# A float32 attention block on one core: the first group's setup reordered across five engines

## The chip, the cores and the metric

The kernel runs on one core of a Trainium2 chip. Its time is the device time of one execution, in microseconds (us). Five engines run their own instruction streams and meet only at semaphores: TensorE (PE), VectorE (DVE), ScalarE (ACT), GpSimd (POOL) and SyncE (SP), which only issues transfers. ACT issues some transfers too.

## The reference, cut to what matters

The input x has 64 batches of 128 tokens with 512 features. There are 16 query heads of 64, and one key and one value head, shared by all.

```
xn  = layernorm(x) * g_in
q   = xn @ Wq   (16 heads of 64), scaled by 64 ** -0.5
k,v = xn @ Wkv, with one null key and null value put in front (null_kv = cond_64[0], cond_64[1])
sim = q k^T + [null_attn_bias[h], attn_bias[h]]; causal and by-batch masks set entries to -max
out = softmax(sim) v;  out = out @ Wo;  y = layernorm(out) * g_out;  return x + y
```

The mask is a row per batch, attn_bias is 16 x 128 x 128 and shared by all batches.

## The kernel before, in words

Two batches make a group (32 groups), two groups a pair (16 pairs). Every matrix product is made of three with float32r operands: high part by high part, high by low, low by high. So each weight has to be split once into a high part (a rounding copy, times g_in for Wq and Wkv) and a low part (the difference). `wq_high(i)` on ACT and `wq_low(i)` on DVE split quarter i of Wq in four instructions each; a quarter serves two of the eight Q tiles of a group. `wo_high(i)` is on ACT, `wo_low(0)` and `wo_low(1)` on POOL, `wo_low(2)` and `wo_low(3)` on DVE.

Of a group PE makes: x turned (8 transposes, in the first two groups only; later groups are turned by 16 small transfers and one DVE transpose, `split_x` and `turned`), the key and value tile ("kv"), eight Q tiles, scores of two tiles at a time (`scores`), values (`values`), and the output projection of each batch (`project_out`). A "tile" is four heads of one batch: a group has eight of them, numbered t = 0 to 7 here. For each tile POOL adds the mask to the bias (`bias`), DVE adds the bias to the scores and takes the row maximum (`logits`), ACT takes exponentials (`soft`), DVE inverts the sums (`inverse`), POOL multiplies (`normalize`), and DVE transposes the weights for the product with v (`turn`).

The bias must first be prepared in place by POOL, once, in two halves (`make_bias(0)`, `make_bias(1)`): subtract the null bias of the head, add the causal mask.

There is no scheduler: each engine's order is written out by hand, and every engine runs its list strictly in order. The loop over pairs has a peeled first pair, ahead of which every engine has its own `first_group()`. PE's list there ends with the last Q tile of the second group that is made early, (1, 5), a wait for Wo's low parts, and `project_out(0)`, L559. What sets that: DVE's `heads_lo(0, g)`, which stand in DVE's list behind `turned(BY_PE)` (x of group 2, turned), which waits for the 16 transfers of `split_x(BY_PE)` on SP, which wait for ACT's `x_norm(BY_PE, 0)`. BY_PE is 2. After this point the pipeline has its steady order.

The loads ahead of the first group: SP issues x of group 0, Wkv, the four quarters of Wq, eight parts of attn_bias (four of 128 KB, the lower 64 rows in 512-byte runs, and four of 64 KB, the upper-left blocks in 256-byte runs), x of group 1, its mask, then Wo. ACT issues g_in, the null key and value, the mask of group 0, and the null bias in two transfers whose runs are 8 bytes long, each read by 64 partitions. PE multiplies an identity 30 times (WARM) while nothing is there for it.

Of the kernel before, what the change touches and what calls it, by code (L numbers as in the profile page):

```python
# [11 lines left out]
P = 128  # L12
# [8 lines left out]
WP = 4  # L21
# [37 lines left out]
WARM = 30  # L59
# [9 lines left out]
def attention_block(nc, x, attn_bias, null_kv, mask, g_in, null_bias, wq, wkv, wo, g_out, out):  # L69
# [4 lines left out]
    with ExitStack() as ctx:  # L74
# [21 lines left out]
        bias_c = sb("bias_c", [P, CB, BOT + TOP])  # L96
        nb_row = sb("nb_row", [P, CB, 2])
# [69 lines left out]
        ld_cols, ld_rows = sem("ld_cols"), sem("ld_rows")  # L167
# [13 lines left out]
        filled = sem("filled")  # L181
        waits_taken = sem("waits_taken")
        wkv_hi_made, wkv_lo_made = sem("wkv_hi_made"), sem("wkv_lo_made")
        wq_hi_made, wq_lo_made, wo_hi_made = sem("wq_hi_made"), sem("wq_lo_made"), sem("wo_hi_made")
# [26 lines left out]
        COL_LOADS, ROW_LOADS, BIAS_LOADS, V_LOADS = 4, 2, 8, 8  # L211
# [78 lines left out]
        def bank_of(slot, kind, i):  # L290
            return ps_proj[(slot + (i if kind == "x" else USE[kind, i])) % 2]

        def proj_count(f, kind, i):

            before = USES * f + XT * (min(f, BY_PE - 1) + 1 if isinstance(f, int) else BY_PE)
            return before - XT + i + 1 if kind == "x" else before + USE[kind, i] + 1

        def halves_of(f, slot, i, from_pe):

            k = slice(KX * i, KX * (i + 1))  # L300
            if from_pe:
                turned = bank_of(slot, "x", i)[:]
            else:
                turned = x_turned[:, k].rearrange("p k n -> p (k n)")
            return turned, *(xt[:, slot, k].rearrange("p k n -> p (k n)") for xt in (xt_hi, xt_lo))

        def front_parts(p, t, first, last):
            if t >= CP:
                return
            for kind, i, ahead in FRONT.get(t % CG, ()):  # L310
                if last and t // CG + ahead == 2:
                    continue
                yield 2 * p + t // CG + ahead, (t // CG + ahead) % 2, kind, i

# [3 lines left out]
        def _(sp):  # L318
# [56 lines left out]
            for i in range(WP):  # L375
                sp.dma_start(raw_piece(i, KT), wq_piece(wq.rearrange("(k p) n -> p k n", p=P), i)).then_inc(ld_wq[i], 16)
            by_head = attn_bias.rearrange("(c u e) i j -> u e i c j", u=2, e=2)
            for u in range(2):
                up = slice(HALF * u, HALF * (u + 1))
                for e in range(2):  # L380
                    sp.dma_start(bias_c[up, :, N * e:N * (e + 1)], by_head[u, e, HALF:N]).then_inc(ld_bias, 16)
                    sp.dma_start(bias_c[up, :, BOT + HALF * e:BOT + HALF * (e + 1)],
                                 by_head[u, e, 0:HALF, :, 0:HALF]).then_inc(ld_bias, 16)
            load_x(0, 1)
            load_mask(0, 1)
# [50 lines left out]
        def _(pe):  # L436
# [66 lines left out]
            def front(f, slot, kind, i):  # L503
                ps = bank_of(slot, kind, i)
                by_pe = isinstance(f, int) and f < BY_PE
                if kind == "x":
                    wait(pe, q_made, QT * f - XT + i + 1)
                    if i == 0:
                        wait(pe, xn_made, GB * (f + 1))
                    for j in range(KX * GB):  # L510
# [787 lines left out]
```

## Time and profile before

| | us |
|---|---|
| median of 3 runs | 1069.09 |
| the three runs | 1069.54, 1069.09, 1062.03 |
| the profiled execution | 1064.88 |
| its span | 1063.0 |
| mean granted TensorE clock over the span | 0.989 of full |

The profiled execution lies between the runs. Its span begins at the first instruction; 1.9 us lie around it. All times of instructions below count from the span's start. Busy time is the time an engine had an instruction in work; what stands behind an arrow in brackets is how long the engine had been idle before the instruction and what ended that.

### The profile page before, as it was taken

The numbers are of one execution on the slowest core, as the hardware profiler recorded it, in microseconds if no ns is written. First come the engines' busy times: TensorE is split into PE (matmuls) and PEld (weight loads), VectorE is DVE, ScalarE is ACT, GpSimd is POOL, SyncE is SP. The second block draws the span as 40 slices with busy tenths as digits, with TensorE's granted clock in tenths as the row PEclk, the third lists the DMA queues.
The fourth block names the chain that finished last, engine by engine and source line by source line (L and its number), as shares of the span: only waits on it lengthen the run. The fifth ranks groups of instructions, "written<-read, shape, count | busy, mean of one in ns | idle before, by whom it ended". The sixth has DMA issues, their size and how long they took to land.

```text
span 1063.0 us, 42980 instructions
## 1 busy us (share of the span) xinstructions
PE 1029.5 (97%) x14254; PEld 902.9 (85%) x14254; DVE 765.8 (72%) x3513; ACT 661.2 (62%) x2620; POOL 828.9 (78%) x1488
## 2 busy tenths in 40 slices
PE   6789999999999999999999999999999999999986
PEld 6678898888888888888888888888888889889875
DVE  4777777777777777786777787776777777777663
ACT  5655675666675665675665676565676565666552
POOL 2867887778878778878778788788788778787775
PEclk8999999999999999999999999999999999999998
DMA  7312222232222222222223122223222223121101
GB/s 213 124 34 86 77 81 89 67 94 76 63 85 82 74 87 73 68 84 85 76 82 91 50 87 84 86 70 89 62 78 85 83 73 93 54 84 59 50 25 60
DMA packets 90013, 84.01 MB, mean 79 GB/s; under 512 B 21568, under 2 KB 64064, under 8 KB 89792
## 3 DMA queue, kind: packets, MB, share of 16 engines
q1 hardware_dynamic: 88336, 81.03, 25.3%
q8 instruction: 138, 2.26, 0.9%
q14 instruction: 83, 0.68, 0.2%
q10 hardware_dynamic: 1456, 0.04, 0.1%
HBM read 40.11 MB, written 16.78 MB: 54 GB/s over the span
## 4 chain that ended last, share of the span: by engine, by line
PE 89%; issue 2%; POOL 2%; ACT 2%; DVE 1%; POOLq 0%; DVEq 0%; ACTq 0%
PE ps_proj L500 38%; PE ps_pv L488 33%; PE ps_s L452 9%; PE ps_pv L477 9%; ACT exp_bot L914 1%; POOL w_nrm L1112 1%; ACT exp_top L914 1%; POOL y_out L1156 0%; POOL y_nrm L1152 0%; DVE logit_bot L608 0%; DVE o_lo L630 0%; POOL bias_b L1103 0%; ACT xn L942 0%; POOL small L1138 0%; DVE wt L624 0%
## 5 line engine op out<-in xcount | busy, mean ns | idle before, releaser
L914 ACT ACTIVATE exp_bot<-logit_bot,neg_max 128x129 f32<-128x129 f32 x512 | 201.6, 399 | 252.0 <-DVE neg_max L608 223.0
L1103 POOL TENSOR_TENSOR bias_b<-bias_c,mask_add 128x256 f32<-128x256 f32 (+1 forms) x512 | 291.9, 599 | 45.3 <-DVE neg_max L608 45.2
L500 PE MATMUL ps_proj<-xt_hi,wq_hi 128*128 128x256 f32 x1024 | 302.5, 295 | 7.5 <-DVE q_sb L690 6.0
L500 PE MATMUL ps_proj<-xt_lo,wq_hi 128*128 128x256 f32 x1024 | 288.6, 282 | 0.9 <-issue 0.9
L500 PE MATMUL ps_proj<-xt_hi,wq_lo 128*128 128x256 f32 x1024 | 288.6, 282 | 0.0
L608 DVE CUSTOM_DVE_ANT_0 logit_bot<-ps_s,bias_b 128x128 f32<-128x128 f32 x512 | 128.3, 288 | 180.1 <-PE ps_s L452 162.4
L500 PEld LDWEIGHTS ps_proj<-xt_hi,wq_hi 128*128 128x128 f32 x1024 | 193.3, 189 | 24.9 <-issue 13.0
L1112 POOL TENSOR_TENSOR w_nrm<-exp_bot,w_inv 128x256 f32<-128x256 f32 x256 | 156.9, 613 | 65.2 <-DVE w_inv L617 65.2
L488 PE MATMUL ps_pv<-wo_hi,o_hi 128*128 128x512 f32 x488 | 199.0, 408 | 1.2 <-DVE o_lo L630 1.2
L488 PE MATMUL ps_pv<-wo_lo,o_hi 128*128 128x512 f32 x488 | 193.5, 397 | 0.0
L500 PEld LDWEIGHTS ps_proj<-xt_hi,wq_lo 128*128 128x128 f32 x1024 | 193.4, 189 | 0.0
L488 PE MATMUL ps_pv<-wo_hi,o_lo 128*128 128x512 f32 x488 | 193.4, 396 | 0.0
L500 PEld LDWEIGHTS ps_proj<-xt_lo,wq_hi 128*128 128x128 f32 x1024 | 193.3, 189 | 0.0
L914 ACT ACTIVATE exp_top<-logit_top,neg_max 128x65 f32<-128x65 f32 x512 | 172.6, 342 | 0.0
L630 DVE SCALAR_TENSOR_TENSOR o_lo<-ps_pv,small,o_hi 128x256 fp32r<-128x256 f32 x252 | 104.5, 477 | 43.3 <-ACT o_hi L923 43.3
L624 DVE STREAM_TRANSPOSE wt<-w_nrm 128x384 f32<-128x384 f32 x256 | 131.8, 553 | 2.0 <-POOL w_nrm L1112 2.0
L452 PEld LDWEIGHTS ps_s<-keys,q_sb 64*64 64x64 f32 x4096 | 98.2, 134 | 37.8 <-issue 29.3
L690 DVE COPY q_sb<-ps_proj 128x256 f32<-128x256 f32 x252 | 105.8, 420 | 33.8 <-PE ps_proj L500 32.4
L923 ACT ACTIVATE o_hi<-ps_pv,small 128x256 fp32r<-128x256 f32 x252 | 98.3, 473 | 37.9 <-PE ps_pv L477 37.9
L452 PE MATMUL ps_s<-keys,q_sb 64*64 64x128 f32 (+1 forms) x4096 | 115.5, 251 | 5.7 <-DVE q_sb L690 2.0
L1112 POOL TENSOR_TENSOR w_nrm<-exp_top,w_inv 128x128 f32<-128x128 f32 x256 | 116.2, 454 | 0.0
L488 PEld LDWEIGHTS ps_pv<-wo_hi,o_hi 128*128 128x128 f32 x488 | 91.9, 188 | 26.8 <-issue 1.4
(94 smaller groups left out, 1778.6 us busy)
## 6 DMA issues: line engine op xcount, KB each, us to landing
x_in<-in_x_dram SPq DMA_DIRECT2D x32, 512.0 KB, 4.1
x_res<-in_x_dram SPq DMA_DIRECT2D x64, 256.0 KB, 2.9
out_dram<-y_out SPq DMA_DIRECT2D x64, 256.0 KB, 2.1
x_split<-xn SPq DMA_DIRECT2D x480, 32.0 KB, 1.9
v_rep<-v_raw SPq DMA_DIRECT2D x256, 32.0 KB, 1.9
w_raw<-in_L_cond_Wq_dram SPq DMA_DIRECT2D x4, 512.0 KB, 11.7
w_raw<-in_L_cond_Wo_dram SPq DMA_DIRECT2D x4, 512.0 KB, 5.2
mask_u<-in_mask_BxS_bk_dram SPq DMA_DIRECT2D x31, 32.0 KB, 3.7
```

The lines of the kernel that those rows point to most:

```text
L452: mm = pe.matmul(scored[HALF * u:HALF * (u + 1)], q_sb[rows, slot, t % CB + s, u, from_:from_ + HALF], keys[rows, slot, b, 0:N if late els ...
L477: mm = pe.matmul(of_tile(ps_pv[g])[DH * e:DH * (e + 1), :, late], v32[rows, slot, b, j], wt[rows, b, block], start=(r == 0), stop=(r == le ...
L488: mm = pe.matmul(out_bank(batch)[:], o[:, u, c], w[:, 2 * c + u], start=(u == 0 and j == 0), stop=(u == 1 and j == len(todo) - 1))
L500: mm = pe.matmul(ps[:, 0:TOK], w[:, k, cols], xt[:, slot, k], start=(j == 0), stop=(j == len(todo) - 1))
L608: ins = nc.vector.tensor_tensor_reduce(out_[:, e, 0:keys_], ps_s[e][:, from_:from_ + keys_], bias[:, e], -1.0, 0.0, ALU.add, ALU.min, neg_ ...
L624: nc.vector.transpose(wt[:, par, :, c], w_nrm[:, s]).then_inc(wt_made, 1)
L630: nc.vector.scalar_tensor_tensor(out=place_of(lo, g), in0=of_tile(ps_pv[g]), scalar=nv_col[:, 0:1], in1=place_of(hi, g).bitcast(F32), op0= ...
L690: nc.vector.tensor_copy(q_sb[:, slot, i // 2, i % 2], bank_of(slot, kind, i)[:, 0:TOK]).then_inc(q_made, 1)
L914: ins = nc.scalar.activation(out_[:, s, j], in_[:, s, j], ACT.Exp, bias=neg_max[:, s, k:k + 1], scale=-1.0, accum_out=w_sum[:, s, k:k + 1])
L923: nc.scalar.activation(place_of(hi, g), of_tile(ps_pv[g]), ACT.Identity, bias=nv_col[:, 0:1]).then_inc(o_hi_made, 1)
L1103: ins = nc.gpsimd.tensor_tensor(out_, bias, key_mask, ALU.add)
L1112: ins = nc.gpsimd.tensor_tensor(out_, w_exp[:, s, :, 0:keys_], w_inv[:, s, 2 * i:2 * i + 2].unsqueeze(2).to_broadcast([P, 2, keys_]), ALU. ...
```

## The change

1. **Null bias.** Instead of two transfers in 8-byte runs, one transfer brings all 16 values to each of the 128 partitions (`nb_all`, 64-byte runs); DVE puts them into `nb_row` with two copies behind `mask_of(0, 0)`, and POOL waits for these (`nb_made`).
2. **Table first.** ACT makes a small copy right behind the issue of g_in, so that its table load comes there and not at the first use.
3. **Loads.** The four 128 KB parts of attn_bias are issued by ACT, behind that copy and ahead of the null bias, null key and value and mask. SP issues Wq quarters 0 and 1, the four 64 KB parts of the bias, Wq 2, x of group 1, Wq 3, its mask.
4. **GpSimd splits part of Wq.** POOL makes the high part of quarter 1 (four instructions, ahead of `make_bias(0)`). DVE takes `wq_low(1)` ahead of the first Q copy.
5. **PE.** 50 identity products in place of 30, ten more behind the transposes; x is turned batch by batch, as soon as one batch is normalized, into two banks of their own (`ps_pv[1]`, `ps_pv[2]`); the first group's kv tile takes its eight products of the high part before it waits for the low part of x; group 1 is turned ahead of Q tile 6, not behind `scores(0, 2)`.
6. **Order of ACT, DVE and POOL in `first_group()`.** ACT: `x_norm(1, 1)` ahead of `soft(0)`, the four `wo_high` later, `x_norm(BY_PE, 0)` behind `soft(5)` (it was ahead of `soft(2)`), with `soft(6)`, `wo_high(3)`, `soft(7)` behind it. DVE: the statistics of group 1 ahead of the second Q copy, `logits(0, 0)` and `logits(1, 1)` ahead of `wq_low(3)`, `x_low_of(1)` ahead of the statistics of group 2, `wo_low(2)` and `wo_low(3)` later. POOL: `x_rstd_of(1)` between `bias(0)` and `bias(1)`.

```diff
-WARM = 30
+WARM = 50
+WARM_X = 10
...
+        def x_bank(i):
+            return ps_pv[1 + i]
...
+            load_wq(0)
+            load_wq(1)
             for u in range(2):
                 for e in range(2):
+                    load_bias_early(sp, u, e)
+            load_wq(2)
             load_x(0, 1)
+            load_wq(3)
             load_mask(0, 1)
...
+            def turn_x(f):
+                for b in range(GB):
+                    wait(pe, xn_made, GB * f + b + 1)
+                    for k in range(KT):
+                        j = GB * (k % KX) + b
+                        bank = x_bank(k // KX)[:, N * j:N * (j + 1)]
+                        mm = pe.transpose(bank, xn[:, b, P * k:P * (k + 1)], ident[:])
+                        if b == GB - 1 and k % KX == KX - 1:
+                            mm.then_inc(x_by_pe, 1)
...
             def first_group():
                 for _ in range(WARM):
                     pe.transpose(ps_s[0][:, 0:P], ident[:], ident[:])
-                for i in range(XT):
-                    front(0, 0, "x", i)
-                front(0, 0, "kv", 0)
+                turn_x(0)
+                for _ in range(WARM_X):
+                    pe.transpose(ps_s[0][:, 0:P], ident[:], ident[:])
+                key_values_of_first()
                 for i in range(4):
                     front(0, 0, "q", i)
                 scores(0, 0)
-                for i in range(4, QT):
-                    front(0, 0, "q", i)
+                front(0, 0, "q", 4)
+                front(0, 0, "q", 5)
+                turn_x(1)
+                front(0, 0, "q", 6)
+                front(0, 0, "q", 7)
                 scores(0, 2)
-                for i in range(XT):
-                    front(1, 1, "x", i)
                 front(1, 1, "kv", 0)
...
+            dve.wait_ge(ld_cols, 16 * COL_LOADS)
             nc.vector.tensor_scalar(k_shift[:], nk_col[:], -SCALE, None, ALU.mult).then_inc(shifts_made, 1)
             nc.vector.tensor_scalar(v_shift[:], nv_col[:], -1.0, None, ALU.mult).then_inc(shifts_made, 1)
             mask_of(0, 0)
+            dve.wait_ge(ld_rows, 16)
+            for u in range(2):
+                up = slice(HALF * u, HALF * (u + 1))
+                nc.vector.tensor_copy(nb_row[up], nb_all[up].rearrange("p (c u e) -> p u c e", u=2, e=2)[:, u]).then_inc(nb_made, 1)
...
                 x_low_of(0, True)
                 wq_low(0)
+                wq_low(1)
                 q_copies(0, 0)
-                wq_low(1)
+                x_stats_of(0, 1)
+                x_mean_var_of(1)
                 q_copies(0, 1)
                 wq_low(2)
                 q_copies(0, 2, 3)
+                logits(0, 0)
+                logits(1, 1)
                 wq_low(3)
-                logits(0, 0)
-                x_stats_of(0, 1)
-                x_mean_var_of(1)
-                logits(1, 1)
                 inverse(0, 0)
+                x_low_of(1, True)
                 x_stats_of(1, 0)
                 x_mean_var_of(2)
...
+            act.wait_ge(filled, 1)
+            nc.scalar.copy(y_shift[:], eps_col[:]).then_inc(table_loaded, 1)
+            for u in range(2):
+                for e in range(2):
+                    load_bias_late(act, u, e)
+            act.dma_start(nb_all[:], null_bias.partition_broadcast(P)).then_inc(ld_rows, 16)
...
-                for i in range(1, WP):
-                    wq_high(i)
-                wo_high(0)
-                q_copies(4)
-                soft(0)
-                q_copies(5, 6)
-                x_norm(1, 1)
-                q_copies(7)
-                soft(1)
-                wo_high(1)
-                x_high_of(1, True)
-                x_norm(BY_PE, 0)
-                soft(2)
+                wq_high(2)
+                wq_high(3)
+                x_norm(1, 1)
+                soft(0)
+                q_copies(4)
+                soft(1)
+                q_copies(5)
+                x_high_of(1, True)
+                q_copies(6, 7)
+                wo_high(0)
+                soft(2)
                 front(1, 1, "kv", 0)
                 soft(3)
+                wo_high(1)
+                soft(4)
                 wo_high(2)
-                soft(4)
+                soft(5)
+                x_norm(BY_PE, 0)
+                soft(6)
                 wo_high(3)
...
+                pool.wait_ge(ld_gin, 16)
+                pool.wait_ge(ld_wq[1], 16)
+                for k in range(KT):
+                    nc.gpsimd.tensor_scalar(wq_piece(wq_hi, 1)[:, k], raw_piece(1, KT)[:, k], gin_col[:, k:k + 1], None,
+                                            ALU.mult).then_inc(wq_hi_by_pool, 1)
+                pool.wait_ge(nb_made, 2)
                 pool.wait_ge(ld_bias, 16 * BIAS_LOADS)
                 make_bias(0)
                 bias(0)
+                x_rstd_of(1)
                 bias(1)
                 make_bias(1)
-                x_rstd_of(1)
```

## Rows read from the trace of the kernel before

**Rows 1.** Busy time by engine, 62 to 1020 us: PE, PEld, DVE, ACT, POOL, clock, DMA

```profile
62.00:1020.00 958.00, 955.28 (x13346) 838.51 (x13346) 705.36 (x3268) 604.77 (x2427) 766.13 (x1376) 1.00 0.25 76
```

**Rows 2.** Timeline of PE to 63 us: start, duration, instructions, idle before them

```profile
1.53 5.83 PE L535 MATMUL ps_s<-ident 128*128 128x128 f32 x30 [1.53 <-POOL ident L1163]
...
11.88 1.97 PE L512 MATMUL ps_proj<-ident,xn 128*128 128x128 f32 x8 [4.51 <-ACT xn L942]
...
15.34 0.55 PE L500 MATMUL ps_proj<-xt_hi,wkv_hi 128*128 128x256 f32 x1 [1.49 <-DVE xt_lo L670]
...
59.20 0.39 PE L500 MATMUL ps_proj<-xt_hi,wq_hi 128*128 128x256 f32 x1 [1.81 <-DVE q_sb L690]
...
62.07 0.47 PE L488 MATMUL ps_pv<-wo_hi,o_hi 128*128 128x512 f32 x1 [1.18 <-DVE o_lo L630]
```

**Rows 3.** Timeline of DVE, 21 to 61 us

```profile
21.57 1.67 DVE L712 SCALAR_TENSOR_TENSOR wq_lo<-w_raw,small,wq_hi 128x256 fp32r<-128x256 f32 x4 [0.58 <-ACT wq_hi L992]
...
23.49 3.61 DVE L712 SCALAR_TENSOR_TENSOR wq_lo<-w_raw,small,wq_hi 128x256 fp32r<-128x256 f32 x4
...
30.95 0.28 DVE L608 CUSTOM_DVE_ANT_0 logit_bot<-ps_s,bias_b 128x128 f32<-128x128 f32 x1
...
34.35 1.25 DVE L651 BATCH_NORM_STATS2 x_stats<-x_in 128x6 f32<-128x512 f32 x2
35.52 0.42 DVE L658 BATCH_NORM_AGGREGATE x_mv<-x_stats 128x2 f32<-128x6 f32 x2
...
40.75 0.69 DVE L670 TENSOR_TENSOR xt_lo<-ps_proj,xt_hi 128x512 fp32r<-128x512 f32 x1 [0.16 <-ACT xt_hi L953]
...
59.94 1.23 DVE L664 STREAM_TRANSPOSE x_turned<-x_split 128x1024 f32<-128x1024 f32 x1
```

**Rows 4.** Timeline of ACT, 7 to 42 us

```profile
7.57 1.28 ACT L984 ACT_TABLE_LOAD   x1 [7.57 <-DMA y_nrm<-in_L_cond_Wkv_dram]
...
13.88 0.58 ACT L953 CAST xt_hi<-ps_proj 128x512 fp32r<-128x512 f32 x1 [0.21 <-PE ps_proj L512]
...
31.48 0.41 ACT L914 ACTIVATE exp_bot<-logit_bot,neg_max 128x129 f32<-128x129 f32 x1 [0.63 <-DVE neg_max L608]
...
32.93 0.76 ACT L1003 COPY q_sb<-ps_proj 128x256 f32<-128x256 f32 x2
...
40.62 1.52 ACT L942 ACTIVATE xn<-x_in,small 128x512 f32<-128x512 f32 x2
```

**Rows 5.** Timeline of POOL, 23 to 46 us

```profile
23.27 1.80 POOL L1180 TENSOR_TENSOR bias_c<-bias_c,nb_row 128x512 f32<-128x512 f32 x2 [14.68 <-DMA bias_c<-in_fside_16xSxS_dram]
...
36.90 0.20 POOL L1120 TENSOR_TENSOR small<-x_mv,small 128x2 f32<-128x2 f32 x1
...
44.83 1.14 POOL L1103 TENSOR_TENSOR bias_b<-bias_c,mask_add 128x256 f32<-128x256 f32 x2
```

**Rows 6.** Timeline of SP's queue: issues, first start and time of all

```profile
6.71 2.23 SPq L381 DMA_DIRECT2D bias_c<-in_fside_16xSxS_dram  x1
...
45.20 10.90 SPq L344 DMA_DIRECT2D x_split<-xn  x16
```

**Rows 7.** DMA queues, 9 to 11 us: packets, MB, share

```profile
q1 hardware_dynamic: 230, 0.23, 33.7%
q10 hardware_dynamic: 212, 0.01, 5.4%
```

**Rows 8.** The same, 15 to 17 us

```profile
q1 hardware_dynamic: 825, 0.73, 105.6%
```

**Rows 9.** DMA issues: KB each, median us to landing

```profile
x_split<-xn SPq DMA_DIRECT2D x480, 32.0 KB, 1.9
...
mask_u<-in_mask_BxS_bk_dram ACTq DMA_DIRECT2D x1, 32.0 KB, 7.1
```

**Rows 10.** Busy time by engine, 9 to 10 and 20 to 21 us, as Rows 1

```profile
9.00:10.00 1.00, 0.00 (x0) 0.00 (x0) 0.00 (x0) 0.87 (x3) 0.00 (x0) 0.89 0.43 134
...
20.00:21.00 1.00, 1.00 (x10) 1.00 (x10) 0.42 (x1) 1.00 (x3) 0.00 (x0) 0.99 1.27 201
```

More of the change, by code:

```diff
@@ L290, in bank_of @@
         def bank_of(slot, kind, i):
-            return ps_proj[(slot + (i if kind == "x" else USE[kind, i])) % 2]
+            return ps_proj[(slot + USE[kind, i]) % 2]
         def proj_count(f, kind, i):
-            before = USES * f + XT * (min(f, BY_PE - 1) + 1 if isinstance(f, int) else BY_PE)
-            return before - XT + i + 1 if kind == "x" else before + USE[kind, i] + 1
+            return USES * f + USE[kind, i] + 1
+        def x_bank(i):
+            return ps_pv[1 + i]
         def halves_of(f, slot, i, from_pe):
@@ L301, in halves_of @@
             if from_pe:
-                turned = bank_of(slot, "x", i)[:]
+                turned = x_bank(i)[:]
             else:
@@ L504, in front @@
                 ps = bank_of(slot, kind, i)
[L505 to L510, printed above, removed]
-                        k, b = KX * i + j // GB, j % GB
-                        mm = pe.transpose(ps[:, N * j:N * (j + 1)], xn[:, b, P * k:P * (k + 1)], ident[:])
-                elif kind == "kv":
-                    if isinstance(f, int) and f == 0:
-                        pe.wait_ge(wkv_lo_made, KT)
-                    if not by_pe:
-                        wait(pe, q_made, QT * f - 1)
+                by_pe = isinstance(f, int) and f == 0
+                if kind == "kv":
+                    wait(pe, q_made, QT * f - 1)
                     wait(pe, xt_lo_made, XT * (f + 1))
@@ L530, in front, with key_values_of_first @@
                 mm.then_inc(proj_done, 1)
+            def turn_x(f):
[7 more added lines that the diff above has]
+                            mm.then_inc(x_by_pe, 1)
+            def key_values_of_first():
+                ps = bank_of(0, "kv", 0)
+                pe.wait_ge(wkv_lo_made, KT)
+                pe.wait_ge(xt_hi_made, XT)
+                for w in (wkv_hi, wkv_lo):
+                    for k in range(KT):
+                        pe.matmul(ps[:, 0:TOK], w[:, k], xt_hi[:, 0, k], start=(w is wkv_hi and k == 0), stop=False)
+                pe.wait_ge(xt_lo_made, XT)
+                for k in range(KT):
+                    mm = pe.matmul(ps[:, 0:TOK], wkv_hi[:, k], xt_lo[:, 0, k], start=False, stop=(k == KT - 1))
+                mm.then_inc(proj_done, 1)
             def first_group():
@@ L751, in first_group @@
                 logits(2, 2)
-                x_low_of(1, True)
                 logits(3, 3)
@@ L755, in first_group @@
                 inverse(2, 2)
+                inverse(3, 3)
                 mask_of(1, 1)
-                wo_low(2)
-                inverse(3, 3)
                 q_copies(1, 0)
@@ L764, in first_group @@
                 inverse(4, 4)
-                wo_low(3)
                 inverse(5, 5)
@@ L768, in first_group @@
                 spread_v_of(0, 0)
+                wo_low(2)
                 logits(6, 6)
@@ L774, in first_group @@
                 q_copies(1, 4)
+                wo_low(3)
                 inverse(7, 7)
@@ L934, in x_norm @@
                 if isinstance(f, int) and 0 < f <= BY_PE:
[L935 removed]
+                    wait(act, x_by_pe, XT * f)
                 if not (isinstance(f, int) and f <= BY_PE):
@@ L948, in x_high @@
                 if from_pe:
-                    wait(act, proj_done, proj_count(f, "x", i))
+                    wait(act, x_by_pe, XT * f + i + 1)
                 else:
```

44 lines of the change are left out of this document (22 added, 22 removed).

## The prediction

> **What bounds the kernel now.** I read the busy time first. From 62 to 1020 us PE has an instruction in work for 955 of 958 us at the full clock [rows 1]; nothing in the change touches that stretch, so the time ends when it ends, and an edit of the beginning is worth exactly what it moves the start of that stretch, up to the losses of the clock. The marker of that start is `project_out(0)`, whose first product runs at 62.07 [rows 2]. Call it P. Ahead of it PE is not the bound: it waits for x, for Q copies, for DVE. So the second reading is of the other engines' timelines backward from P, and the question is which chain ends last there, before and after.
>
> Before, P waits for DVE's low part of the first heads [rows 2], behind `turned(BY_PE)` at 59.94 [rows 3]. From there to P are 2.13 us, whatever comes ahead. `turned` needs the 16 transfers that SP issued from 45.20 on in 10.90 us [rows 6], 1.9 us each to landing [rows 9]: they had landed by about 57.5, some 2.4 us before they were used. They start when ACT has normalized group 2, which it did at 40.62 to 42.1 [rows 4]. So there is a chain of fixed length: from the end of `x_norm(BY_PE, 0)` to P it takes 0.1 + 10.9 - 0.6 (the last issue's own time) + 1.9 + 2.1 = 14.4 us. Before, it had slack.
>
> **The change, part by part.**
>
> Null bias and load order. While the 8-byte runs are in the queue of ACT's loads (q10), the queue of SP's loads (q1) gets one packet for each of theirs: 230 against 212 in 9 to 11 us, 0.23 MB [rows 7]. Once they are gone it moves 825 packets and 0.73 MB in the same time [rows 8]. 512 such runs at 106 a us are 4.8 us; 128 runs of 64 bytes at that rate are 1.2. Saved: 3.6 us of slow loading. The bias also no longer stands behind Wq 2 and 3 (1 MB, 2.8 us at the fast rate). POOL started on it at 23.27 [rows 5]; I expect 15 to 17, held at the end by the split of Wq 1 or by `nb_made`. That is the largest thing the change does, but before the change this was not late: `logits(0, 0)` at 30.95 [rows 3] stood in DVE's list behind `wq_low(3)`, which ran up to it.
>
> Table first. The load took 1.28 us at 7.57, when Wkv had landed [rows 4]. It goes to a time in which ACT has nothing to do: up to 1.28 us. Against it, Wkv now shares turns with 512 KB of bias on the other queue; that they alternate one for one is what rows 7 show. I price that at 0 to 1.3 us. Either way PE's 50 identities end at 1.53 + 50 x 0.194 (5.83 us for 30) = 11.2 [rows 2], and PE turns x only then, against 11.88. The transposes then run at the full clock, 1.0 us in place of 1.97 [rows 2], so ACT's two casts of the high part (0.58 each [rows 4]) end at about 13.3, not 14.5, and the high part of Wq 0 is there at 15.0, not 16.1. Early gain: 1.1 us. The Trainium skill (DMA: Bandwidth & Descriptors, Issuing engines are not separate DMA queues) says that transfers of different issuers run on the same 16 engines and interleave; rows 7 agree, and by it splitting the bias between ACT and SP buys no bandwidth.
>
> DVE's list. Two new waits stand in it ahead of `x_low_of(0)`: the null key and value, and the null bias, with the mask between. They are queued on ACT's transfers behind four bias loads. The mask landed 7.1 us behind its issue [rows 9], at 10.2. With four issues of at least 0.5 us ahead that becomes 12.2; if their 1024 packets must first go out one for one beside SP's, at 412 a us for both, it becomes 15.2. Behind DVE's wait stand the low part of x, so PE's kv tile, and every low part of Wq. So `wq_low(0)` starts between 15.0 and 17.3.
>
> Then the price of the early bias. Four low-part instructions on DVE took 1.67 us with POOL idle and 3.61 us with POOL in the bias preparation [rows 3, 5]. Now Wq's split on POOL, `make_bias(0)` and `bias(0)` run from about 12.5 to 20, just beside `wq_low(0)` and `wq_low(1)`. The Trainium skill (SBUF — State Buffer, Who interferes with whom) says that a DVE instruction with two SBUF inputs and a GpSimd instruction that reads SBUF exclude each other for the whole instruction; the trace agrees by 1.67 against 3.61. This is the rule that speaks against the change: it moves POOL's work from beside one part of DVE's splits to beside another. The price of POOL's own four instructions is not in the trace for this form; it is hidden on POOL as long as the bias lands later.
>
> The sum to the first logits, L: DVE does three low parts (5.0 us free, 10.8 locked), four Q copies of 0.38, statistics 1.25 + 0.42, then PE's scores, 1.1. From 15.0 with nothing locked L = 15.0 + 5.0 + 1.5 + 1.7 + 1.1 = 24.3. From 17.3 with everything locked it is 32.4. POOL's bias work lasts an estimated 4.7 us at a time (1.80 for a subtraction pair, at most as much for the causal pair, 1.14 for a tile's bias [rows 5]), so about half is locked, and the mask lies between its ends: I take L = 28.0, 3 us earlier than 30.95.
>
> The sum from L to P. In the new order: exponentials start 0.53 behind L (31.48 against 30.95 [rows 3, 4]); `soft(0)` 1.45, one Q copy 0.38, `soft(1)` 1.45, a Q copy 0.38 [rows 4]; two casts 1.16; low part 0.69, statistics of group 2 1.67 [rows 3]: 7.9 with semaphores. Then POOL's `x_rstd_of(BY_PE)`, `bias(3)`, `normalize(1, 1)`, `bias(4)`, `wo_low(0)`, `normalize(2, 2)`, `bias(5)`: the same seven in the same order ran without a break from 36.90 to 45.97 [rows 5], 9.1. Then `logits(5, 5)`, `soft(5)` and, now behind it, `x_norm(BY_PE, 0)`: 0.5 + 1.5 + 1.5 = 3.5. Then 14.4. Together P = L + 34.9. Before, the normalization came 9.7 us after L; it now comes 19.0 after it. With L = 28.0, P = 62.9: 0.8 us later than before. The 3 us gained are given back in a queue of SP which had slack.
>
> The rest, PE's products up to the last early Q tile (59.20 before [rows 2]), is not on that chain: it moves up with L and with the later Wo copies, to 54 to 57. So PE now stands idle for 5 us or more ahead of P, against 1.18. What that does to the clock the rows show: idle from 7.36 on, PE's grant had fallen by 10 us (0.89 in that slice), and it was at the half level from the kv tile at 15.34 to just before 20 [rows 2, 10]. Half rate for 4.6 us of work costs 2.3 us, and P is where PE becomes the bound: it counts in full. Bounds: 0 to 2.3; I take all of it.
>
> WARM_X, the kv tile's early start and the early transposes of group 1 all lie ahead of a waiting engine: nothing each, since DVE's splits or the chain above cover them; uncovered WARM_X would cost 1.9.
>
> **Sum**, against the profiled execution (1064.88, of it span 1063.0): + 0.8 + 2.3 = 1068.0. Its bounds: L = 24.3 gives P = 59.2 and no fall of the clock, 1062.0; L = 32.4 gives P = 67.3 and 1072.4. The runs lie from 1062.03 to 1069.54, mean 1066.9, so the profiled one is 2.0 below their mean; a new median would by that be about 1070, and I give 1069.
>
> **Rivals.**
>
> Faster: the gain is carried. The mask lands early, DVE finds POOL waiting at its splits, L is 24.3, and P is then ahead of 59.2; if `logits(5, 5)` doesn't wait for POOL either, the chain loses 2 us more: 1060. For it: POOL's list has idle time before the statistics, and rows 3 show 1.67 whenever POOL waits. Against it: that needs DVE's three splits all outside of POOL's 15 us of bias work. 0.28.
>
> Nothing of it matters: the locks and the later mask take back the early gain, the transfers of x keep their old slack, P stays within 1 us, the clock stays: 1065. 0.17.
>
> Slower: ACT's issues back up. SP's first bias issue took 2.23 us because its queue was full [rows 6]. If ACT's four do the same (6.9 us more than at 0.5), ACT is free for the high part of Wkv at about 15, not 8, and x is normalized 6 us later than now; everything behind moves: L about 35, P 70, with the clock 1075. It decides from the point at which ACT's issues end behind Wkv's landing, 7.6 us. Against it: ACT's queue holds far fewer packets than SP's did. 0.10.
>
> The forecast, a little slower, 1066 to 1073: 0.45.
>
> **Chances.** Over 1% (10.7 us) is about what a measurement of this kernel tells from no change. Only the slow rival's tail gets past it upward (0.05); only more than the faster rival's working does so downward (0.06). Within it: 0.89. The range takes in the faster rival and most of the slow one: 1060 to 1075.
>
> **What would show it.** Right: `x_split`'s 16 issues start at 48 us or later and `turned` waits for them; PE idle ahead of P for 5 us and the grant at half behind it; POOL's first bias instruction at 15 to 17; a run of four low parts at over 3 us beside it; first logits at 27 to 29. Wrong: `turned` directly behind `inverse(7, 7)` with no wait; or the first scores not behind DVE's Q copies. The prediction fails most if `logits(5, 5)` is not held by POOL, since the whole length from L to P rests on that run of seven.

## The result and the profile after

After the change the median is 1092.16 us (4 runs, 1090.38 to 1101.64), before in the same job 1067.82 (4 runs, 1062.03 to 1069.54): ratio 1.0244, 95% interval 1.0175 to 1.0312. The change costs 24.3 us, and the forecast of 1069, with its whole range, was wrong. The record lists a fifth run of after, 1087.68, that the median leaves out; with it the median would be 1091.92. The profiled execution of after is its longest run, 1101.64 us, and its span is 1099.8. Of all runs below only one counts as slow, that of 1114.57 us in experiment 8.

First the beginning. The timeline of PE, to 66 us (start, duration, instructions, in brackets the idle time before them and its releaser):

```profile
1.53 8.57 PE L566 MATMUL ps_s<-ident 128*128 128x128 f32 x50 [1.53 <-POOL ident L1204]
9.94 1.18 PE L547 MATMUL ps_pv<-ident,xn 128*128 128x128 f32 x8
...
17.17 0.78 PE L560 MATMUL ps_proj<-xt_lo,wkv_hi 128*128 128x256 f32 x4 [3.84 <-DVE xt_lo L703]
20.43 0.58 PE L519 MATMUL ps_proj<-xt_hi,wq_hi 128*128 128x256 f32 x1 [2.48 <-DVE wq_lo L752]
...
65.68 0.76 PE L507 MATMUL ps_pv<-wo_hi,o_hi 128*128 128x512 f32 x1 [6.42 <-DVE o_lo L663]
```

The timeline of DVE:

```profile
13.54 0.15 DVE L738 TENSOR_SCALAR small<-small 64x1 f32<-64x1 f32 x1 [3.45 <-DMA small<-in_cond_dram]
...
14.70 0.29 DVE L708 TENSOR_SCALAR mask_add<-mask_u 128x256 f32<-128x256 uint8 x1 [0.95 <-DMA mask_u<-in_mask_BxS_bk_dram]
14.91 0.89 DVE L744 COPY nb_row<-nb_all 64x8 f32<-64x8 f32 x2
...
17.04 5.13 DVE L752 SCALAR_TENSOR_TENSOR wq_lo<-w_raw,small,wq_hi 128x256 fp32r<-128x256 f32 x8
...
25.77 1.67 DVE L752 SCALAR_TENSOR_TENSOR wq_lo<-w_raw,small,wq_hi 128x256 fp32r<-128x256 f32 x4
...
29.88 0.29 DVE L641 CUSTOM_DVE_ANT_0 logit_bot<-ps_s,bias_b 128x128 f32<-128x128 f32 x1 [1.31 <-PE ps_s L471]
...
63.53 1.25 DVE L697 STREAM_TRANSPOSE x_turned<-x_split 128x1024 f32<-128x1024 f32 x1 [5.32 <-DMA x_split<-xn]
```

The timeline of ACT:

```profile
1.26 1.28 ACT L1012 ACT_TABLE_LOAD   x1 [1.26 <-PEq L1334]
...
11.90 1.71 ACT L1033 ACTIVATE wq_hi<-w_raw,small 128x256 fp32r<-128x256 f32 x4
...
49.36 1.51 ACT L982 ACTIVATE xn<-x_in,small 128x512 f32<-128x512 f32 x2
```

That of POOL, and that of SP's queue:

```profile
12.00 3.78 POOL L1241 TENSOR_SCALAR wq_hi<-w_raw,small 128x256 fp32r<-128x256 f32 x4 [3.14 <-DMA w_raw<-in_L_cond_Wq_dram]
15.88 1.61 POOL L1221 TENSOR_TENSOR bias_c<-bias_c,nb_row 128x512 f32<-128x512 f32 x2
```

```profile
51.02 11.20 SPq L361 DMA_DIRECT2D x_split<-xn  x16
```

Most of what was forecast for the beginning is there. The bias starts at 15.88, not 23.27 [rows 5]; the first logits come at 29.88, not 30.95 [rows 3]; x of group 2 is normalized 19.5 us behind them, `x_split`'s issues start at 51.02, not 45.20 [rows 6], DVE waits 5.32 us for them, and P is 65.68, not 62.07 [rows 2]. The order of events is the forecast one; the first logits and P come later than forecast (28.0 and 62.9). In the busy time by engine (columns as Rows 1) the clock around P is low, and then comes a part for which the prediction had no term:

```profile
60.00:70.00 10.00, 4.32 (x12) 3.49 (x13) 5.98 (x13) 1.14 (x2) 0.69 (x4) 0.55 0.16 43
...
200.00:1020.00 820.00, 792.29 (x11082) 693.12 (x11081) 580.41 (x2711) 501.32 (x2009) 639.50 (x1143) 0.98 0.25 75
```

Far behind the changed code, PE stands idle for 27.7 of 820 us; before, the same stretch has 819.05 busy. A turn of the loop over pairs, from one row of first scores to the same row of the next turn, took 63.2 to 63.7 us before. Now the first of the 14 turns, the only one with no jump back ahead of it, takes 62.5 us and the others 64.4 to 68.9. What PE waits for is in the view of waits (us in total, times, the longest), the two rows of the loop:

```profile
PE ps_proj L519 <- issue: 24.2, 13, 2.3
...
PE ps_pv L496 <- issue: 4.7, 7, 1.6
```

"issue" is no engine and no transfer: all semaphores had been met. The timeline of PE shows where in the turn it stands, once a turn behind the same scores:

```profile
234.16 0.90 PE L471 MATMUL ps_s<-keys,q_sb 64*64 64x128 f32 x32 [0.17 <-issue]
237.18 0.39 PE L519 MATMUL ps_proj<-xt_hi,wq_hi 128*128 128x256 f32 x1 [2.12 <-issue]
```

These are the scores right behind the jump back to the loop's first instruction. The DMA queues of that moment, 234.3 to 234.5 us, have one packet of the queue that brings instructions (packets, MB, share), 2.7 to 2.9 us ahead of the product at 237.18. The view does not say for which engine it is:

```profile
q8 instruction: 1, 0.02, 44.6%
```

Before has the same packet at the same place behind its jump, 228.2 to 228.4 us, and PE works through it: its products at 228.89 and 229.11 follow with no gap.

```profile
q8 instruction: 1, 0.02, 43.8%
```

Over the span that queue moves this much (the page's part on queues), 16.4 KB a packet:

```profile
q8 instruction: 139, 2.28, 0.9%
```

The wait itself is not the whole cost. Two turns, busy time as above, the first with a wait of 1.80 us, the second with waits of 1.71 and 1.57, and two us of the second:

```profile
299.00:363.38 64.38, 62.58 (x889) 54.73 (x889) 46.85 (x218) 40.46 (x162) 51.38 (x93) 1.00 0.26 77
626.40:695.32 68.92, 65.63 (x888) 57.58 (x889) 46.89 (x218) 40.46 (x162) 51.00 (x93) 0.95 0.25 72
...
630.00:632.00 2.00, 2.00 (x12) 2.00 (x11) 0.02 (x1) 0.00 (x0) 0.00 (x0) 0.50 0.72 200
```

In eight of the 13 turns behind a jump the granted clock fell to its half level for some us behind a wait (mean of the turn 0.95 to 0.975), in five it did not. By an estimate from these means (one less the clock, times the turn's length, summed) that is 15 us of the profiled execution, beside 29 us of idle time in the 14 turns. The other runs of after had a mean clock of 0.981 to 0.986, not 0.974, and are 9 to 14 us shorter.

So the first theory was: PE's instructions come in blocks; where a block ends, relative to the jump, depends on how many PE instructions stand ahead of the loop, and the change adds 60 of them (20 identities for WARM and 10 for WARM_X, each a weight load and a product).

### The profile page after: what moved, and what is told of

The parts are those of the page before. It is cut to its first block, busy times and chain, and to the rows that moved or that the text cites. A ratio compares the mean times of both kernels' runs of the same rounds, so it can differ in the third digit from the quotient of the medians.

```text
span 1099.8 us, 43042 instructions
## 1 busy us (share of the span) xinstructions
PE 1036.3 (94%) x14284; PEld 906.1 (82%) x14284; DVE 761.6 (69%) x3515; ACT 660.2 (60%) x2617; POOL 836.6 (76%) x1492
## 3 DMA queue, kind: packets, MB, share of 16 engines
q1 hardware_dynamic: 87248, 80.51, 24.4%
## 4 chain that ended last, share of the span: by engine, by line
PE 86%; issue 6%; POOL 4%; ACT 1%; DVE 1%; SPq 1%; DMA 1%; ACTq 0%; POOLq 0%; DVEq 0%
PE ps_proj L519 36%; PE ps_pv L507 32%; PE ps_s L471 9%; PE ps_pv L496 9%; SPq L361 1%; POOL bias_b L1144 1%; POOL w_nrm L1153 1%; DMA mask_u<-in_mask_BxS_bk_dram 1%; POOL y_out L1197 0%; POOL y_nrm L1193 0%; ACT exp_bot L954 0%; DVE o_lo L663 0%; POOL bias_c L1221 0%; ACT exp_top L954 0%; POOL bias_c L1226 0%
## 5 line engine op out<-in xcount | busy, mean ns | idle before, releaser
L519 PE MATMUL ps_proj<-xt_hi,wq_hi 128*128 128x256 f32 x1024 | 305.1, 298 | 32.3 <-issue 24.2
L1144 POOL TENSOR_TENSOR bias_b<-bias_c,mask_add 128x256 f32<-128x256 f32 (+1 forms) x512 | 296.1, 608 | 42.1 <-DVE neg_max L641 40.9
L519 PEld LDWEIGHTS ps_proj<-xt_hi,wq_hi 128*128 128x128 f32 x1024 | 199.6, 195 | 49.1 <-issue 37.1
L519 PEld LDWEIGHTS ps_proj<-xt_hi,wq_lo 128*128 128x128 f32 x1024 | 200.1, 195 | 0.0
L519 PEld LDWEIGHTS ps_proj<-xt_lo,wq_hi 128*128 128x128 f32 x1024 | 200.0, 195 | 0.0
L507 PEld LDWEIGHTS ps_pv<-wo_hi,o_hi 128*128 128x128 f32 x488 | 92.0, 189 | 34.7 <-issue 6.7
```

What stands on the lines that cost most here:

```text
L507: mm = pe.matmul(out_bank(batch)[:], o[:, u, c], w[:, 2 * c + u], start=(u == 0 and j == 0), stop=(u == 1 and j == len(todo) - 1))
L519: mm = pe.matmul(ps[:, 0:TOK], w[:, k, cols], xt[:, slot, k], start=(j == 0), stop=(j == len(todo) - 1))
L1144: ins = nc.gpsimd.tensor_tensor(out_, bias, key_mask, ALU.add)
```

## The experiments

"Before" was timed again beside each group of runs: 1065.92, 1067.35, 1066.41 and 1066.59 us for the four groups.

**1. Sixty PE instructions more, nothing else.**

```diff
-WARM = 30      (in before)
+WARM = 60
```

> The kernel before with one number changed: 60 identity products ahead of the first group in place of 30, which puts 60 PE instructions (30 weight loads, 30 products) ahead of PE's loop, as many as the change does. Nothing else moves. Theory 'place of the loop': PE's instructions are fetched in blocks of 16 KB, and with its loop 60 instructions later in its block the sequencer runs dry once in each turn of the loop, as in the changed kernel (1.55 to 2.26 us idle of PE before the first Q product behind the first scores, 13 times). It expects 1085 to 1095, a wait of about 2 us called issue in each of the 13 turns, and a loop turn of 64.5 to 67 us in place of 63.4. Theory 'order': the loss of the loop comes from the reordered first group (what state it leaves the loop in). It expects 1067 to 1070, at most 1.5 us more than before for the later end of the identity products, and turns of 63.4 us.

Measured 1100.63 us, ratio 1.031 (1.0282 to 1.0339): 34.7 us for 30 identities on an engine that has nothing else to do then. The waits inside the loop are the same two as in after, and P is no later than before (61.12):

```profile
PE ps_proj L500 <- issue: 24.8, 13, 2.3
...
PE ps_pv L477 <- issue: 3.6, 5, 0.9
```

**2. The change without its sixty.**

```diff
-WARM = 50      (in after)
-WARM_X = 10
+WARM = 30
+WARM_X = 0
```

> The changed kernel with 30 identity products ahead in place of 50, and none in place of 10 behind the transposes: its PE loop then lies where it lay in the kernel before, to within the instruction. All the reordering stays. Theory 'place of the loop' expects the 13 waits of the loop gone, turns of 63.4 us, and only the beginning's loss left: 1070 to 1075 (3.6 us later start of project_out(0), some 2 us of half clock). Theory 'order' expects 1088 to 1095 with the waits still there.

Measured 1056.74 us, ratio 0.9906 (0.9882 to 0.993), turns of 62.4 to 63.3 us: the loss is gone, and 9 us more with it, which neither theory had foreseen. P is 64.47, 1.2 us earlier than in after, so the identities' own time can be at most about that much of the 35.4 us between the two.

**3. The change with 256 instructions more than before.** 118 small transposes behind WARM (32 x 32) in the kernel of experiment 2, with WARM_X at its 10.

> The changed kernel with 196 more PE instructions ahead of its loop (30 in place of 50 large identity products, and 118 transposes of 32x32 behind them), so that 256 more than in the kernel before stand there: 256 instructions of 64 bytes are one block of 16 KB. If it is the place within a block, the waits of the loop go and the time is 1070 to 1076, as with 60 fewer. If it is the mere number of instructions ahead, or the later start, they stay or grow: 1090 or more.

Measured 1057.9 us, ratio 0.9923 (0.9902 to 0.9944), turns of 62.4 to 63.3, P 65.73. 196 more instructions than after cost nothing but give back 34 us. So not their number counts but where they put the loop, and 256 more is as none. That fits a block of one packet, 16.4 KB, if an instruction has 64 bytes.

**4. Thirty and 128 more.** Before with WARM = 45, and before with 64 small transposes (32 x 32) behind WARM.

> The kernel before with 45 identity products in place of 30: 30 PE instructions more ahead of the loop, half of what the change adds. Sixty cost 35 us. The cost of place should set in where the rest of the first block behind the loop's target has been used before the next block is there: PE's wait with 60 is about 1.9 us, and 30 instructions are 1.8 us of Q products. So with 30 the wait is near 0 to 0.4 us a turn: 1066 to 1075. If the loss came in proportion, 1083; if it is all or nothing by some other boundary, 1066 or 1100.

> The kernel before with 64 transposes of 32x32 behind the 30 identity products: 128 PE instructions more ahead of the loop, half a block of 16 KB. The place of the loop's target in its block is then on the other side. If only the part of the block behind the target counts, the first block would end inside of the products or at the scores: 1090 or more if it is the shorter part, about 1066 if the target has passed into the next block and finds nearly all of it. By the run with 60, the target lies 64 to 90 instructions ahead of the block's end there, so with 128 it would be 0 to 25 ahead of it: nearly nothing left, a longer wait than with 60, 1100 or more.

Thirty: 1088.25 us, ratio 1.0214 (1.0161 to 1.0267); 128: 1117.42, ratio 1.0466 (1.0423 to 1.0509). With thirty the wait is in another place, in the values:

```profile
PE ps_pv L477 <- issue: 15.6, 13, 2.0
```

With 128 it comes right behind the jump, 2.9 us in the mean of 13 turns, and is longest (first the waits, then one in the timeline):

```profile
PE ps_s L452 <- issue: 40.0, 14, 3.4
```

```profile
236.39 1.46 PE L452 MATMUL ps_s<-keys,q_sb 64*64 64x128 f32 x32 [3.23 <-issue]
```

One packet of instructions starts between 233.6 and 233.7 us, inside that wait and 2.7 to 2.8 us ahead of the scores:

```profile
q8 instruction: 1, 0.02, 67.4%
```

This gives a rule for this loop; it was made after these runs and fits them, and no later run tested it. With 128 more the block ends at the jump's target, or a few instructions behind it, and PE waits for the whole time that the next block takes to come, 2.9 us in the mean and 3.23 in the row above. So in before the block ends about 128 instructions behind the target, that is behind 64 of scores (0.83 us) and 64 of Q products (32 x 0.117 = 3.7 us): 4.6 us of work, more than 3.2, no wait. With 60 more it ends 68 behind, just after the scores: 2.9 - 0.83 = 2.0 us by the rule, 1.86 measured in the mean (24.2 by 13).

The second kind of wait shows where the blocks lie. Counted in the traces from the jump's target, in weight loads and products, it stands at instruction 310 with 60 more, at 340 with 30 more, and at 370 in before and with 256 more: it moves by just the instructions that were added. PE goes through the values, instructions 200 to 360, fastest of all (160 in 1.57 us). A block's end inside them cost 1.2 us a turn with thirty more; ten instructions behind them, as in before, it cost 0.3 us in three turns of 13. What the place in the values costs was read, not forecast: on record stood 1066 to 1075 for the thirty, and 1088.25 is a miss. With 128 more the idle time in the 14 turns is 37 us and the clock takes an estimated 17, again by its mean in each turn.

**5. The 9 us more: the tile.** `nb_all` is 64 bytes in each partition and is allocated ahead of `nb_row`, so every tile behind it moves by 64 bytes. Before with such a tile, unused:

```diff
+        nb_all = sb("nb_all", [P, H])
         nb_row = sb("nb_row", [P, CB, 2])
```

> The kernel before with the 64-byte tile nb_all allocated and not used, ahead of nb_row: every later SBUF tile lies 64 bytes further on in its partition, as in the changed kernel. Theory 'addresses' (the loop's loss comes from SBUF addresses) expects 1085 to 1095. The two others expect the time of the kernel before, within 0.5%.

Measured 1053.02 us, ratio 0.9886 (0.9858 to 0.9914): 13 us faster with not one instruction changed. The groups by line and form, 200 to 1020 us (count, then busy time and mean ns of one), show which: each product of 256 columns is 4 to 5 ns shorter, those of 512 columns are not. Before:

```profile
L500 PE MATMUL ps_proj<-xt_hi,wq_lo 128*128 128x256 f32 x825 | 232.1, 281 | 0.0
...
L488 PE MATMUL ps_pv<-wo_hi,o_lo 128*128 128x512 f32 x416 | 164.8, 396 | 0.0
```

With the unused tile:

```profile
L501 PE MATMUL ps_proj<-xt_hi,wq_lo 128*128 128x256 f32 x832 | 230.1, 277 | 0.0
...
L489 PE MATMUL ps_pv<-wo_hi,o_lo 128*128 128x512 f32 x416 | 164.8, 396 | 0.0
```

216 such products a turn by 4.5 ns are 1.0 us, by some 16 turns 15 us; measured 13. No theory on record had this: 'addresses' was to cost some 20 to 30 us, the others to change nothing.

**6. The other steps of the address.** The same with 32, 96 and 128 bytes.

> The kernel before with an unused tile of 32 bytes ahead of nb_row. By the sizes of the tiles ahead of them the high and low parts of x begin 96 bytes past a multiple of 128 in the kernel before, and 32 past one with the 64-byte tile; here they begin at a multiple. If the cost comes from rows of x that begin late in a line of 128 bytes, this is as fast as with 64, 1053, or faster; if it is the multiple of 64 or 32 itself that decides, another value comes out: 1067 or a third time.

> Before with an unused tile of 96 bytes ahead of nb_row: the last of the four 32-byte steps. With 0 bytes 1066, 32 bytes 1062, 64 bytes 1053, 128 bytes 1067. If what counts is how far the operands lie from the old place within 128 bytes, it is like 32 bytes: 1060 to 1064. If it counts whether the start lies 64 bytes from the slow place only: 1066. If 64 and 96 both count as the fast half: 1053.

> The kernel before with an unused tile of 128 bytes ahead of nb_row. The tile of 64 bytes took 13 us off (1053.0), with every 256-column product into ps_proj 4.8 ns shorter start to start. If what counts is where the tiles of x's parts lie within 128 bytes, this kernel is as slow as the kernel before, 1067; if any shift away from the old place does it, or a period longer than 128 bytes, 1053.

| bytes | 0 | 32 | 64 | 96 | 128 |
|---|---|---|---|---|---|
| us | 1066.4 | 1062.35 | 1053.02 | 1060.6 | 1067.17 |
| ratio to before | 1 | 0.9965 (0.9949 to 0.9982) | 0.9886 (0.9858 to 0.9914) | 0.9929 (0.9906 to 0.9952) | 1.0004 (0.9992 to 1.0017) |

128 bytes are as none; before stands at the slow end and half way round is the fast one. The guess on record, that x is read fastest where its parts begin at a multiple of 128 bytes, failed (32 bytes). Nor is it one kind of product alone: at 96 bytes those of 256 columns are back at 281 ns and those of 512 columns are at 392 to 393, not 396. Only tiles behind `nb_row` moved, x turned among them, not Wq and Wo. Which of these addresses it is and why, no run here tells.

**7. The order of the beginning alone.** The kernel of experiment 2 with `nb_all` allocated last: old place of the loop, old addresses.

> The kernel after with WARM 30, WARM_X 0 and nb_all allocated behind all other tiles: the loop stands where it stood before, and every tile that products read has its old address. What is left of the change is the order of the beginning. Additive theory: before + 3.7 us (1056.7 - 1053.0, the same pair at the shifted addresses), so 1069 to 1071, each 256-column product of the loop as long as before, turns of 63.2 to 63.7 us. Rival, the order touches the loop too: then the turns or the waits in it differ from before's, and the time isn't 3 to 5 us above before. Rival, addresses matter through nb_row's or bias_c's neighbours, not through the products' operands: 1057.

Measured 1068.67 us (11 runs), before 1066.59 (15 runs), ratio 1.0017 (1.0006 to 1.0029): 2.1 us slower. Its P is 65.46, behind 5.56 us of idle time (forecast 62.9 and 5 or more), and of all waits for "issue" the longest is 1.0 us:

```profile
65.46 0.77 PE L507 MATMUL ps_pv<-wo_hi,o_hi 128*128 128x512 f32 x1 [5.56 <-DVE o_lo L663]
```

**8. The change without its shift of addresses.** After with `nb_all` allocated last.

> The kernel after with one edit: nb_all allocated behind all other tiles. The place of the loop stays as changed (60 PE instructions later), the addresses are before's. Additive theory: 1092.2 + 13 = 1105, so 1102 to 1108, with waits for nothing of about 29 us in all. Rival, the shift gave nothing in this kernel since its loop is bound by the fetch: 1090 to 1094.

Measured 1105.25 us (4 runs, 1098.05 to 1114.57), ratio 1.0337 (1.0293 to 1.0382). Without the longest of them the median is 1100.53. By the two ratios to before it is 10 us above after, give or take 9: the shift is worth something in this kernel too, near the 13 us of the tile alone, but the times can't size it. The first turn of the loop, which has no jump ahead of it and no wait, gives a size: 62.50 us in after and 63.27 here, as 62.55 with the unused tile and 63.25 in before. 0.77 us by 16 turns are 12.

**9. The chain that sets P: the normalization earlier.** In the kernel of experiment 2:

```diff
                 soft(3)
+                x_norm(BY_PE, 0)
                 wo_high(1)
...
                 soft(5)
-                x_norm(BY_PE, 0)
                 soft(6)
```

> The changed kernel with its PE loop at the old place (60 fewer identity products' instructions, as in the run a_less60, 1056.7 us), and the normalization of group 2 on ACT moved back from behind soft(5) to behind soft(3), ahead of wo_high(1). The prediction's chain (end of x_norm(BY_PE, 0), 16 issues of SP, turned, project_out) says that this alone holds the first project_out at 64.5 us with PE idle for 5.5 us ahead of it and a fall of the clock behind it. If so, project_out starts at 60 to 61, the clock does not fall, and the time is 1049 to 1051, 6 to 7 us less. If the order of the rest is at fault (DVE's list, POOL's share), project_out moves by under 1.5 us and the time stays at 1055 or more.

Measured 1052.36 us, ratio 0.9855 (0.9816 to 0.9895), 4.4 us below experiment 2. The first two rows are SP's transfers, now and for the next group; then PE's:

```profile
46.76 11.13 SPq L361 DMA_DIRECT2D x_split<-xn  x16
...
68.57 11.86 SPq L361 DMA_DIRECT2D x_split<-xn  x16
```

```profile
61.36 0.47 PE L507 MATMUL ps_pv<-wo_hi,o_hi 128*128 128x512 f32 x1 [1.14 <-DVE o_lo L663]
...
88.07 0.58 PE L519 MATMUL ps_proj<-xt_hi,wq_hi 128*128 128x256 f32 x1 [2.20 <-DVE q_sb L723]
```

P is 3.1 us earlier and DVE no longer waits for the transfers, so the chain was what held it. The time is 1.4 us above what was expected (1049 to 1051), and a second wait stands at 88.07, for x of the next group. It takes back part of what P gave: the loop starts 1.5 us earlier, not 3.1. This wait is an old one. Before had it too, and in experiment 2 it was gone, where P came late:

```profile
88.24 0.39 PE L500 MATMUL ps_proj<-xt_hi,wq_hi 128*128 128x256 f32 x1 [1.35 <-DVE q_sb L690]
```

**10. That second wait.** The statistics of group 3 on DVE ahead of `turned(BY_PE)`, its normalization on ACT ahead of the high part of group 2.

> The run a_norm (1052.4 us) with the same chain of the next group started earlier: DVE takes the statistics of group 3 ahead of turned(BY_PE), where it used to stand idle, and ACT normalizes group 3 ahead of the casts of group 2. In a_norm the first project_out came 3.1 us earlier than in a_less60, but PE then waited 2.2 us at 88 us for a Q copy and ran part of the next 10 us at half clock: the next group's 16 transfers, issued from 68.6 to 80.4, had become the end of the chain. If that is so, the wait at 88 goes and the time is 1049 to 1050. If the wait has another cause (POOL, DVE), it stays and so does the time, 1052.

Measured 1054.76 us, ratio 0.9894 (0.9873 to 0.9916), no better than experiment 9 and 5 us above what was expected. The wait at 88 is gone (from 80 to 100 us PE is busy for 19.97 of 20), but PE waits longer ahead of P, and the clock is low around it (0.79 from 60 to 80 us). DVE had no idle time left there: in its timeline the statistics run from 58.91 to 60.5 and `turned` starts at 60.43, where it started at 59.22 in experiment 9:

```profile
62.58 0.77 PE L507 MATMUL ps_pv<-wo_hi,o_hi 128*128 128x512 f32 x1 [3.47 <-DVE o_lo L663]
```

**11. ACT's issues.** In the kernel of experiment 9 the null key and value and the mask are issued ahead of the four bias parts and the null bias.

> The run a_norm with ACT's issues in another order: null key and value and the mask of group 0 first, then the four late bias loads and the null bias. In the changed kernel DVE waited 3.45 us for the null key and value and 0.95 for the mask, and PE 3.84 us for the low part of x behind them, where I had put the mask between 12.2 and 15.2 us; it was there at 14.7. If those waits are on the path, the first logits come 1.5 to 2.5 us earlier than in a_norm and so does project_out, and the time is 1050 to 1051. If the null bias copies on DVE (queued behind the late bias loads too) merely take the place of the wait, nothing moves: 1052.

Measured 1054.07 us, ratio 0.9894 (0.9862 to 0.9925): no gain, another miss. DVE's wait only changes its object (its timeline):

```profile
11.54 0.29 DVE L708 TENSOR_SCALAR mask_add<-mask_u 128x256 f32<-128x256 uint8 x1 [0.32 <-DMA mask_u<-in_mask_BxS_bk_dram]
16.18 0.36 DVE L744 COPY nb_row<-nb_all 64x8 f32<-64x8 f32 x2 [4.35 <-DMA nb_all<-cond_null_attn_bias_dram]
```

**12. The null bias alone.** Before with `nb_all`, its one transfer and its two copies.

> The kernel before with the null bias alone changed: one transfer of whole rows into nb_all, two DVE copies into nb_row, POOL waits for these. It carries the 64-byte shift of all later tiles, so it is to be compared with the run b_tile (1053.0 us). The reading of the 8-byte runs says that the stretch of slow loads from 9 to 15 us shrinks by 3.6 us and POOL starts on the bias at 19 to 20 us, not at 23.3; but nothing before project_out waited for the bias, so the time is that of b_tile, within 2 us. If the bias had been on the path, 1048 to 1050.

Measured 1056.09 us, ratio 0.9893 (0.9854 to 0.9932). That is less than before by the 64 bytes; against the unused tile of the same size (1053.02, another group of runs) it is 3 us more in the medians, and by the ratios to before no difference (0.9893 and 0.9886). POOL's bias starts at 21.95 in place of 23.27, a gain of 1.3 us where 3.3 to 4.3 were expected. P did not gain by it: it is 63.41, with the unused tile 61.80, and no run tells why it is later.

## Why the prediction was wrong

The failed step is its first: "nothing in the change touches that stretch, so the time ends when it ends". PE being busy for 955 of 958 us [rows 1] says what bounds the loop, not that its duration is fixed. Two things touched it which are in no engine's work: the place of its instructions (+34.7 us alone in before; +35.4 in the changed kernel, from 1056.74 to 1092.16, with up to 1.2 us of the identities' own time in it) and the addresses of its tiles (-12.9). With the order's +2.1 the three measured apart from the change make 23.9, against 24.3 measured. The step's second half failed in the text on WARM_X and the identities, "nothing each": it priced their time, and what they cost is the place to which their number moves the loop. The sum had no term for either, so no bound of it could hold the result.

The Trainium skill (Runtime: NRT & Kernel Launch, Instruction fetch mechanics) says that instructions are refilled in blocks of 16 KiB, 256 instructions, that crossing into the next is mostly hidden, and that a taken branch whose target is not in the two pages at hand has to wait for it to be fetched. The block size agrees with experiment 3, and the wait behind the jump with experiment 4 (3.23 us with 128 more). "Mostly hidden" held for before and for +256; at +30 the wait at a block's end far behind the jump was 1.2 us a turn, and at +30, +60 and +128 the total was 21 to 50 us. That page names the mechanism, and I could have read the change against it.

The rest, by its own steps:

- **P as the end of a fixed chain: right.** P itself was forecast at 62.9 and came at 65.68, 1.9 us of it by the later L and 0.9 between L and P. `x_norm(BY_PE, 0)` ends at 50.87, P is 14.8 us behind it, forecast 14.4. Experiment 9 shows it by moving the one step.
- **From L to P: right.** 35.8 us, forecast 34.9.
- **L: too early.** 29.88, forecast 28.0 and "27 to 29". DVE reached `wq_low(0)` at 17.04, within 15.0 to 17.3, and its eight low parts beside POOL took 5.13 us, between 3.3 free and 7.2 locked, as assumed. Missing in the sum was PE: behind its 2.48 us of idle time it made the first Q tiles at the half clock (0.41 us a product until 24.4, 0.28 behind), so DVE's copies waited for it.
- **Table first and the early gain: larger than forecast.** The identities took 0.171 us each, not 0.194, x was turned from 9.94 on, forecast 11.2, and the high part of Wq 0 was there at 13.6, forecast 15.0. It did not matter: DVE was waiting for the null key and value until 13.54 and for the mask until 14.70, in the range given (12.2 to 15.2).
- **The null bias and the loads: right in the end point only.** POOL's first bias at 15.88, forecast 15 to 17, held by its own split of Wq 1 (3.78 us, of which the text had no price). The 3.6 us put on the 8-byte runs were 1.3 when they alone were changed (experiment 12); the rest must have come with the other changes of the loads, which no run takes apart.
- **The clock: right in size, but it did not count in full.** It was 0.55 from 60 to 70 us behind 6.42 us of idle time. In experiment 7 the half level lasted into the first us behind P:

```profile
65.46:68.00 2.54, 2.54 (x6) 2.06 (x7) 2.54 (x7) 0.26 (x1) 0.00 (x0) 0.50 0.19 52
68.00:72.00 4.00, 4.00 (x14) 3.15 (x14) 1.29 (x4) 1.02 (x2) 1.28 (x4) 0.74 0.02 6
```

  That is 2.3 us of lost clock (0.50 x 2.54 + 0.26 x 4.00), as forecast. But the wait of 1.35 us at 88.24, which before has behind P, was gone, so the loop started 3.8 us later than before for a P that was 3.4 later. "P is where PE becomes the bound: it counts in full" was wrong at least by that wait.
- **The sum of all this**, +3.1 against the profiled execution, was measured as +2.1 in experiment 7 (0.6 to 3.1 by its interval) and +3.7 at the shifted addresses (1056.74 against 1053.02). The agreement is in part luck: P alone moved by 3.4 us where 0.8 were forecast, and the clock's 2.3 hardly showed. Of the rivals none happened; that of ACT's issues came near its point (ACT's last issue ends at 7.5 us) without deciding.

## What to carry to other kernels

When a loop is bound by one engine, count the instructions that an edit adds ahead of it on that engine, and read the waits for "issue" and the granted clock inside the loop before and after; if the waits grow, move the loop by idle padding before judging the edit. Compare two versions at the same place and the same addresses, or an edit of 2 us is judged by +35 or by -13. Here the whole reordering with the normalization moved up, which holds the 64 bytes too, is at 1052.36 us, and an unused tile of 64 bytes alone at 1053.02: the order itself is worth about nothing.

## What the runs showed of the hardware

- A jump back in PE's code costs PE up to 3.4 us of waiting a turn, or nothing, by where a block of 256 instructions ends behind its target: 1066, 1088, 1101, 1117 and (after the change, beside 1056.7) 1057.9 us for 0, 30, 60, 128 and 256 instructions more.
- Waits of 1.6 to 2.3 us in an otherwise busy stretch let the granted clock fall to the half level in eight of 13 turns of after, and in five not; such a turn is 1.7 to 4.5 us longer than the shortest of the others, 64.4 us.
- The start address of a tile modulo 128 bytes changes float32 products of 256 columns by 4 to 5 ns each (281 to 277 ns), 1.1% of this kernel, where it is moved by 64 bytes; products of 512 columns stay at 396 ns then, and are 392 to 393 ns where it is moved by 96.
- DVE's wait for ACT's small loads moved from one to the other with the order of the issues: with the mask first the mask was there at 11.54 and the null bias, then last, at 16.18; in after the mask, then last, was there at 14.70 and the null bias by then.
